# Slot feed-forward: eight of the 24 row turns move from the opening into steps 1 and 2, and the row maxima are taken in three parts

## The reference, cut to what matters

```python
def _L1_ffn_ref(x, norm_gamma, slot_norm_gamma, slot_embeds, w1, b1, w2, b2):
    xn = rmsnorm(x, norm_gamma)
    sn = rmsnorm(slot_embeds, slot_norm_gamma)
    logits = jnp.einsum('bnd,esd->bnes', xn, sn)
    dispatch = jax.nn.softmax(logits, axis=1)
    combine = jax.nn.softmax(logits.reshape(b, n, e * s), axis=-1)
    slots = jnp.einsum('bnd,bnes->besd', xn, dispatch)
    h = jnp.einsum('besd,edh->besh', slots, w1) + b1[None, :, None, :]
    h = jax.nn.gelu(h, approximate=False)
    eo = jnp.einsum('besh,ehd->besd', h, w2) + b2[None, :, None, :]
    return jnp.einsum('bmd,bnm->bnd', eo.reshape(b, e * s, DIM), combine)

x = x + _L1_ffn_ref(_layernorm(x, axis=-1), ...)
```

## Time and profile before

| what | value |
|---|---|
| time, median of 3 runs (lowest to highest) | 2077.16 us (2075.8 to 2077.53) |
| profiled execution, first to last instruction | 2078.8 us |
| PE busy over the span | 1838.9 us (88%) |
| DVE busy over the span | 1522.3 us (73%) |
| ACT busy over the span | 1123.1 us (54%) |
| opening of `slot_ffn` (468.80 to 508.40) | 39.60 us, mean PE clock 0.75 |
| step 0 with the row maxima (508.40 to 544.71) | 36.31 us |
| step 1 (544.71 to 566.03) | 21.32 us |
| one later step (566.03 to 591.50) | 25.47 us, PE busy 25.47 us |

### The profile page before, as it was taken

One profiled execution on the slowest core, in us unless ns is written; L12 is line 12 of the kernel. 1 busy time (PEld: TensorE's weight loads), 2 busy tenths in 40 slices (PEclk: granted clock), 3 DMA queues, 4 the chain that ended last, 5 costly groups with the idle time before them and its releaser, 6 DMA issues. The chain is left out here.

```text
span 2078.8 us, 41262 instructions
## 1 busy us (share of the span) xinstructions
PE 1838.9 (88%) x16364; PEld 1345.4 (65%) x16364; DVE 1522.3 (73%) x3187; ACT 1123.1 (54%) x1896; POOL 152.1 (7%) x121
## 2 busy tenths in 40 slices
PE   7969268997899999999999999989897898699995
PEld 6844155665466666677777777656664576598884
DVE  6977877667777777777777776777666666688886
ACT  3535854446366666666655565436531554377672
POOL 0001300000000000000000000000000000144431
PEclk9979689997999999999999999999999998799998
DMA  6120001003100000000000000010001001577775
GB/s 219 46 78 0 0 1 52 3 2 112 31 28 25 21 21 21 22 21 21 21 21 21 1 1 1 1 52 2 23 1 55 1 3 46 172 255 251 247 246 180
DMA packets 80366, 120.92 MB, mean 58 GB/s; under 512 B 9840, under 2 KB 62512, under 8 KB 80048
## 3 DMA queue, kind: packets, MB, share of 16 engines
q1 hardware_dynamic: 75760, 106.22, 15.3%
q0 software_dynamic: 4416, 12.06, 1.6%
HBM read 103.58 MB, written 14.68 MB: 57 GB/s over the span
## 5 line engine op out<-in xcount | busy, mean ns | idle before, releaser
L2547 PE MATMUL sl_ps_eo<-sl_w,sl_hT 128*128 128x256 f16 x3072 | 353.2, 273 | 0.8 <-DVE sl_hT L2790 0.7
L2524 PE MATMUL sl_ps_h<-sl_slot_inT,sl_w 128*128 128x512 f16 x1536 | 338.2, 379 | 0.5 <-ACT sl_h L2667 0.5
L2547 PEld LDWEIGHTS sl_ps_eo<-sl_w,sl_hT 128*128 128x128 f16 x3072 | 298.5, 98 | 35.8 <-DVE sl_hT L2790 1.3
L2667 ACT ACTIVATE sl_h<-sl_ps_h,sl_b1T 128x512 f32<-128x512 f32 x256 | 175.7, 687 | 170.3 <-PE sl_ps_h L2524 163.2
L2524 PEld LDWEIGHTS sl_ps_h<-sl_slot_inT,sl_w 128*128 128x128 f16 x1536 | 150.0, 98 | 176.2 <-ACT sl_h L2667 2.4
L2790 DVE TENSOR_TENSOR sl_hT<-sl_h,sl_hT 128x512 f16<-128x512 f32 x256 | 177.0, 692 | 102.1 <-ACT sl_hT L2670 97.7
L1123 DVE TENSOR_REDUCE at_neg_max<-at_ps 128x8 bf16<-128x1024 f32 x96 | 116.9, 1221 | 79.7 <-PE at_ps L833 79.7
L2086 PE MATMUL mo_ps_h<-mo_xgT,mo_w 128*128 128x256 f16 x1104 | 124.3, 273 | 5.7 <-issue 4.4
L2804 DVE SCALAR_TENSOR_TENSOR sl_result<-sl_ps_eo,sl_b 128x256 f32<-128x256 f32 x128 | 54.3, 424 | 97.6 <-PE sl_ps_eo L2547 93.3
L2097 PE MATMUL mo_ps_eo<-mo_w,mo_hT 128*128 128x256 f16 x1104 | 124.4, 273 | 0.1
L2086 PEld LDWEIGHTS mo_ps_h<-mo_xgT,mo_w 128*128 128x128 f16 x1104 | 107.5, 98 | 19.5 <-issue 7.0
(11 more groups left out here) (433 smaller groups left out, 3640.7 us busy)
## 6 DMA issues: line engine op xcount, KB each, us to landing
mo_w_raw<-in_L_ffn_W SPq DMA_DIRECT2D x46, 1024.0 KB, 7.8
sl_w_in<-in_L_ffn_w SPq DMA_DIRECT2D x16, 1024.0 KB, 5.4
at_ctxT<-ctx_pairs SPq DMA_DIRECT2D x9, 512.0 KB, 7.8
mo_w_raw<-pair_rows SPq DMA_DIRECT2D x4, 1024.0 KB, 9.3
mo_b<-in_L_ffn_b SPq DMA_DIRECT2D x23, 128.0 KB
ac_attention_w<-L_attention_w SPq DMA_DIRECT2D x3, 768.0 KB, 11.9
w_pairs<-ac_w_pair SPq DMA_DIRECT2D x3, 768.0 KB, 3.2
ac_ctx_all<-in_ctx SPq DMA_DIRECT2D x4, 512.0 KB, 8.0
```

The source lines that it names most:

```text
L2524: last = pe.matmul(ps_h[:, j % 2], w1[:, e % 2, w, k, j * P:(j + 1) * P], slot_inT[:, q % 2, x, k].rearrange("p b s -> p (b s)"), start=(k ...
L2547: last = pe.matmul(ps_eo[:, b % 2, 0:D], hT[:, hp, j, b * P:(b + 1) * P], w2[:, e % 2, w, j], start=(j, a) == (0, 0), stop=(j, a) == (HJ - ...
L2667: act.activation(h[:, j % 2], ps_h[:, j % 2], ACT.Gelu, bias=b1T[:, q // G4, j:j + 1], scale=1.0 / W_SCALE).then_inc(h_ready, 1)
```

## The change

`ROWS` is put in another order (x0 to x3, slots 0 to 7, x4 to x15), and the opening turns 16 of the 24 only. Rows 16 to 19 (x8 to x11) are normalised, split, turned and copied out in step 1, rows 20 to 23 (x12 to x15) in step 2. The row maxima come in three parts: those of x0 to x7 beside `hidden(0, j)`, two ahead of each; those of x8 to x11 beside `hidden(1, j)` in step 2, one ahead of each; those of x12 to x15 in the same way in step 3. Each part has its own `turn_row_maxima` and its own copy by ACT. `normal_rest` moves from the opening to the end of DVE's step 1. The cut diff:

```diff
-ROWS = [("x", n) for n in range(B // 2)] + [("slot", e) for e in range(E)] + [("x", n) for n in range(B // 2, B)]
-FIRST_SLOT = B // 2
+ROWS = [("x", n) for n in range(4)] + [("slot", e) for e in range(E)] + [("x", n) for n in range(4, B)]
+FIRST_SLOT = 4
+OPENING = 16
+MAXIMA_PARTS = ((0, 8), (8, 12), (12, 16))
...
+        def rows_of_step(q):
+            return range(OPENING + 4 * (q - 1), OPENING + 4 * q) if q in (1, 2) else ()
+        def maxima_part(q):
+            return q - 1 if 1 <= q <= len(MAXIMA_PARTS) else None
...  (tensor)
             def row_logits(q):
                 n, i = divmod(q, 2)
-                pe.wait_ge(rowsT_ready, NT)
-                enough(pe, rmax_ready, q - 1)
+                part = next(k for k, (lo, hi) in enumerate(MAXIMA_PARTS) if lo <= n < hi)
+                pe.wait_ge(rowsT_ready, E + 4 * (n // 4 + 1))
+                enough(pe, rmax_ready, q - 1 + part)
+                enough(pe, result_ready, 4 * part)
...
-            def turn_row_maxima():
-                pe.wait_ge(rmax_ready, 2 * B + 1)
+            def turn_row_maxima(part):
+                pe.wait_ge(rmax_ready, 2 * MAXIMA_PARTS[part][1] + part + 1)
+                if part >= 1:
+                    pe.wait_ge(out_added, 4 * (part - 1) + 3)
...
             for j in range(HJ):
-                for i in range(4):
-                    row_logits(4 * j + i)
+                for i in range(2):
+                    row_logits(2 * j + i)
+                if j == 0:
+                    pe.wait_ge(rowsT_ready, OPENING)
                 hidden(0, j)
-            turn_row_maxima()
+            turn_row_maxima(0)
             for q in range(1, STEPS):
                 if q > 1:
+                    part = maxima_part(q)
                     for j in range(HJ):
+                        if part is not None:
+                            row_logits(2 * MAXIMA_PARTS[part][0] + j)
                         hidden(q - 1, j)
+                    if part is not None:
+                        turn_row_maxima(part)
                     logits(q)
...
                 turn_dispatch(q)
                 shift(q)
+                for m in rows_of_step(q)[:2]:
+                    pe.wait_ge(h_ready, HJ * q)
+                    turn_row(m)
                 result_of(q - 1, 2)
                 slot_inputs(q)
+                for m in rows_of_step(q)[2:]:
+                    turn_row(m)
                 result_of(q - 1, 3)
...  (vector)
-                if m == FIRST_SLOT + E + AHEAD - B // 2 - 2:
-                    normal_rest(dve, t, env)
...
+            def row_maxima_known(part):
+                lo, hi = MAXIMA_PARTS[part]
+                dve.wait_ge(rmax_ready, 2 * hi + part)
+                enough(dve, rmax_turned, part)
+                dve.tensor_tensor(neg_rmax[:, lo:hi], ...).then_inc(rmax_ready, 1)
...
                     for j in range(HJ):
+                        if maxima_part(q) is not None:
+                            row_maximum(2 * MAXIMA_PARTS[maxima_part(q)][0] + j)
                         rest_of_hidden(q - 1, j)
+                    if maxima_part(q) is not None:
+                        row_maxima_known(maxima_part(q))
...
                 normalise_dispatch(q)
+                for m in rows_of_step(q):
+                    row(m)
                 result_of(q - 1, 1)
                 dispatch_out(q)
+                for m in rows_of_step(q)[:2]:
+                    low_part(m)
                 combine_rest(q)
+                for m in rows_of_step(q)[2:]:
+                    low_part(m)
                 result_of(q - 1, 2)
                 inputs_rest(q)
                 result_of(q - 1, 3)
+                if q == 1:
+                    normal_rest(dve, t, env)
```

More of the change, by code:

```diff
@@ L2465, in turn_row @@
                         at = (a * C + c) * P
-                        last = pe.transpose(ps_rows[m % 3][:, at:at + P], parts[:, a, c * P:(c + 1) * P], ident_h[:])
+                        last = pe.transpose(row_bank(m)[:, at:at + P], parts[:, a, c * P:(c + 1) * P], ident_h[:])
                 last.then_inc(rows_turned, 1)
@@ L2500, in shift @@
                 pe.wait_ge(made_consts, 5)
[L2501 removed]
+                pe.wait_ge(rmaxT_ready, min(max(q, 1), len(MAXIMA_PARTS)))
                 for b in range(4):
@@ L2520, in hidden @@
                     pe.wait_ge(in_split, C * (q + 1))
+                    if rows_of_step(q):
+                        pe.wait_ge(rowsT_ready, rows_of_step(q)[-1] + 1)
                 enough(pe, h_ready, HJ * q + j - 1)
@@ L2554, in _ @@
             pe.wait_ge(made_consts, 2)
-            for m in range(NT):
+            for m in range(OPENING):
                 if m == FIRST_SLOT:
@@ L2616, in turned_out @@
                 to = xrT[:, :, :, i] if kind == "x" else slotsT[:, :, :, i]
-                act.activation(to, ps_rows[m % 3].rearrange("p (a c l) -> p a c l", a=2, c=C), ACT.Copy).then_inc(rowsT_ready, 1)
+                act.activation(to, row_bank(m).rearrange("p (a c l) -> p a c l", a=2, c=C), ACT.Copy).then_inc(rowsT_ready, 1)
             def slot_squares():
@@ L2681, in _ @@
             act.wait_ge(made_consts, 3)
-            for m in range(FIRST_SLOT, NT + 2):
-                if m < NT:
+            for m in range(FIRST_SLOT, OPENING + 2):
+                if m < OPENING:
                     high_part(m)
@@ L2693, in _, with row_maxima_out @@
             weights_high(0, 3)
+            def row_maxima_out(part):
+                act.wait_ge(rmax_turned, part + 1)
+                enough(act, shifted, part + 1 if part else 0)
+                act.activation(neg_rmaxT[:], ps_rmax, ACT.Copy).then_inc(rmaxT_ready, 1)
             for j in range(HJ):
                 hidden(0, j)
-            act.wait_ge(rmax_turned, 1)
-            act.activation(neg_rmaxT[:], ps_rmax, ACT.Copy).then_inc(rmaxT_ready, 1)
+            row_maxima_out(0)
             combine_weights(0)
@@ L2831, in _ @@
             dve.wait_ge(made_consts, 4)
-            for m in range(FIRST_SLOT, NT):
+            for m in range(FIRST_SLOT, OPENING):
                 if m == FIRST_SLOT:
@@ L2852, in _ @@
             dve.wait_ge(cleared, 3)
+            def row_maxima_known(part):
+                lo, hi = MAXIMA_PARTS[part]
+                dve.wait_ge(rmax_ready, 2 * hi + part)
+                enough(dve, rmax_turned, part)
+                dve.tensor_tensor(neg_rmax[:, lo:hi], row_max[:, lo:hi, 0, 0], row_max[:, lo:hi, 1, 0], ALU.min).then_inc(rmax_ready, 1)
             for j in range(HJ + 1):
                 if j < HJ:
-                    for i in range(4):
-                        row_maximum(4 * j + i)
+                    for i in range(2):
+                        row_maximum(2 * j + i)
                 if 1 <= j <= 2:
```

27 lines of the change are left out of this document (20 added, 7 removed).

## The result

| | before | changed |
|---|---|---|
| time, median of 4 runs each on one chip | 2076.48 us (2073.85 to 2077.53) | 2086.20 us (2085.51 to 2089.38) |
| ratio, 95% interval | | 1.0048 [1.0033, 1.0062] |
| profiled execution: span | 2078.8 us | 2083.8 us |
| the block alone, in that execution | 887.58 us | 897.50 us |

The account below looks back on a forecast made before the run. DVE was taken to bound the opening and step 0, PE the full steps from step 2; -18.9 + 4.8 + 8.6 + 3.9 + 6.2 + 3.4 = +8.0 us gave 2085.2 us, range 2076.5 to 2091.5.

Parts of the forecast that it names:

- A: Opening, to the first row maximum: 6.7 us saved in three parts (1.7, 2.0, 3.0), with eight fewer turns and no `normal_rest`.
- B: Step 0, first row maximum to the turn of the maxima: 12.2 us saved, 22.5 instead of 34.7, DVE still the bound.
- third rival: Every gap drops the clock, opening at its poorer end: +15.9 us, 2093.1; chance 0.17.
- C: Step 1, first turned rows: +4.8 us, as PE waits for a low part from DVE and does two more turns.
- D: Step 2, products: +8.6 us for eight row logits, the bank read, a stall behind `normal_rest` and the maxima turn's wait.
- E: Step 2, turned rows: +3.9 us, a wait of 2.95 for the low part plus the turns.
- F: Step 3, products with row logits and the turn of maxima: +6.2 us (0.35 + 3.45 + 2.4).
- G: Low clock behind PE's four new gaps in steps 2 and 3: two low stretches of 1.7 us, +3.4.
- that nothing would be held: Rival: PE's later work passes a waiting turn, so stalls cost nothing; -9.3 us, 2067.9; chance 0.11.
- 9.6 of moved work: Price on PE of the work moved into steps 1 to 3: 16 logits 6.9, eight turns 2.0, two bank reads 0.7.
- the second: Rival: no low clock and the opening at its better end, so no change: +0.5 us, 2077.7; chance 0.20.

Follow-up runs that it names:

- e2: Changed kernel with the first two late turns of steps 1 and 2 behind `result_of(q-1, 2)` on PE instead of ahead of it: 2077.81 us, 1.0013.
- e1: Changed kernel with `normal_rest` on DVE in front of step 1's weights, no longer behind step 1's last addition: 2081.90 us, 1.0041.
- e3: Changed kernel with the second and third turns of row maxima behind the step's logits, `combine(q-2, 3)` and `result_of(q-1, 0)`: 2080.31 us, 1.0015.
- e5: Changed kernel with `normal_rest` early, late turns behind `result_of(q-1, 2)` and later turns of maxima behind `result_of(q-1, 0)`: 2068.51 us, 0.9962.
- e4: Changed kernel with products nobody reads filling PE's new gaps in steps 1 to 3, no wait taken away: 2079.37 us, 1.0024.
- e7: On top of e5, step 1's four rows normalised and split earlier on DVE and turned around `turn_dispatch(1)` and `shift(1)`: 2068.79 us, 0.9961.
- e6: Changed kernel's three-part row maxima alone: all 24 rows turned in the opening with `normal_rest` there, none in steps 1 and 2: 2078.44 us, 1.0014.
- e9: On top of e5, unread products ahead of `hidden(0, 0)`, the first turn of row maxima and `turn_dispatch(1)`: 2068.21 us, 0.9949.

## Why the prediction was right, and where it wasn't

**A and B** held: to the first row maximum -7.08 (-6.7 forecast; its three parts -2.2, -1.8, -3.0 for -1.7, -2.0, -3.0), and step 0's loop -12.09 (-12.2). That B came so near is partly luck: two misses cancel. DVE was busy for 18.87 of the 22.64 us (20.1 forecast) and idle for 3.8 (2.4), since it waited 2.5 us, not 1.8, behind its first two maxima. The near end of A and B was also added up wrongly: 5.0 and 10.7 are -15.7, not -16.5. The forecast doesn't use it; the third rival would come to +16.7.

**C** held: +4.56 for +4.8. The wait is 3.56 (3.7), by the low part that DVE makes at 542.02 (ten instructions stand ahead of it behind the normalised weights, not nine; the sum went by their times). The clock over `result_of(0, 2)` is low as it was before, 3.86 us for 4.29. C left it as it was, and that this was right isn't explained: in e2, with the old gap ahead of it and without the new one, the same products run at 1.00.

**D, E and F** held in every wait: 2.25 and 2.37 (2.4 each), 2.95 (2.95), 2.37 (2.4). Without the clock D comes to 8.9 (8.6), E to 4.2 (3.9), F to 6.5 (6.2). Of the 0.3 over, 0.16 at each gap is the end of the last product ahead of it, which no gap's figure contains (48 products of `hidden` take 10.36 us from the first start to the next group's, 10.52 to their end); in F the read of the result bank adds 0.1 and the turn itself 0.07.

**G was sized too small**: 3.4 for two low stretches in four gaps; there were three, 1.68 + 1.58 + 1.67 = 4.9. That is 1.5 more; with the three times 0.3, and 0.5 less from A to C, +8.0 becomes +9.9. It also made the reading that I gave for step 2 ("some 38 us") wrong: all three low stretches lie in it, and it took 43.5. I had counted gaps of 2.2 to 2.5 us that lost the clock and taken the share. e1, e2 and e3 show that the share doesn't belong to a gap: each changed what an unedited gap cost. So that G came within 1.5 us is luck too, and what decides which gap loses the clock stays open.

The rivals: that nothing would be held was priced at -9.3 and is refuted for this kernel, but e5 realises it: with the waits gone the block is 9.45 shorter. So the 9.6 of moved work fits, too: 9.92 were paid there. The third rival (every gap drops the clock) was nearer than the second, but not met: step 3's gap left the clock up, A and B saved 19.2 and not 16.5, and C's low stretch was no longer than before. What the Trainium skill says ("TensorE: Matmul & The Clock Gate", section "What's actually happening"), that sustained activity lifts the clock, agrees with e4, where fillers alone won 5.8 us.

## What to carry to other kernels

Work that moves from a stretch where another engine is the bound into one where the tensor engine is busy all the time is paid there at its full price, so place it so that nothing on that in-order engine waits for it: put the step's independent products ahead of it, and make its inputs in an earlier idle stretch of the other engine. The same change was worth +9.7 us and -8 us, with the order of instructions in steps 1 to 3 as the only difference. For such small edits compare the length of the block in the profile, with the granted clock behind each gap, before believing the gain of a single edit: it may be a low stretch that moved.

## What the runs showed of the hardware that I had not expected

- The same gap of 2.37 us ahead of the first turn of maxima left the clock at 1.00 in nine profiles, and in e7 and e6 it was 0.63 and 0.61 behind it; a gap of 2.95 us cost 1.67 us in the changed kernel and nothing in e1 and e3. In two profiles of one program the places were the same.
- Identity products that nobody reads kept the clock at 1.00 across gaps of 2.25 to 2.95 us (e4). Where they started late they gained nothing: in e9 they put `hidden(0, 0)` off by 1.7 us and made it and the logits behind it 1.7 us shorter.
